# GpSimd, not VectorE, multiplies the edge weights of the first layer's gather quads

## The reference, cut to what matters

```python
deg_out = jax.ops.segment_sum(edge_weight, src, num_segments=N_NODES)
deg_in = jax.ops.segment_sum(edge_weight, dst, num_segments=N_NODES)
norm = edge_weight * jax.lax.rsqrt(deg_out[src] * deg_in[dst] + EPS)

def _gcn_layer(x, W, b, src, dst, norm, n_nodes):
    xt = x @ W
    msg = xt[src] * norm[:, None]
    agg = jax.ops.segment_sum(msg, dst, num_segments=n_nodes)
    return jax.nn.relu(agg + b)
h6 = _gcn_layer(h5_all, W6, b6, src, dst, norm, N_NODES)
h7 = _gcn_layer(h6, W7, b7, src, dst, norm, N_NODES)
```

## Time and profile before

| | |
|---|---|
| runs of the kernel before | 3711.46, 3719.69, 4076.07 us; median 3719.69 us |
| profiled execution, own time | 3675.28 us |
| its span in the profile | 3673.5 us, mean granted clock 0.908 |
| busy PE / DVE / ACT / POOL | 82% / 49% / 31% / 59% of the span |
| gathers of layer 1 | 984, from 491.4 us on |

### The profile page before, as it was taken

The page is one execution under the profiler, slowest core; times in us unless marked ns, Lnnn a source line. Parts: engine busy times, 40 slices in busy tenths (PEclk is TensorE's granted clock), DMA queues, the critical chain, the costliest instruction groups (busy, mean ns, idle before and its releaser), DMA issues.

```text
span 3673.5 us, 51374 instructions
## 1 busy us (share of the span) xinstructions
PE 3014.1 (82%) x16152; PEld 1995.3 (54%) x16152; DVE 1801.7 (49%) x4528; ACT 1146.4 (31%) x4063; POOL 2169.9 (59%) x2090
## 2 busy tenths in 40 slices
PE   4778836888888888888875888888888878888998
PEld 3445524555555555555553555556555546555666
DVE  9989835666666666666541332223212324232334
ACT  5788734444444444344320110002000101012211
POOL 4766656766767677676764666666666666630000
PEclk8899968999999999999987989889888989889999
DMA  4331134454545545445465534654554554533221
GB/s 119 99 102 59 52 78 135 152 164 137 179 141 165 153 140 178 136 152 163 129 208 176 150 105 156 202 187 149 193 191 153 187 159 152 189 112 101 81 77 48
DMA packets 219168, 515.12 MB, mean 140 GB/s; under 512 B 62470, under 2 KB 129461, under 8 KB 207799
## 3 DMA queue, kind: packets, MB, share of 16 engines
q0 software_dynamic: 88704, 243.35, 23.2%
q1 hardware_dynamic: 123683, 261.95, 20.9%
q10 hardware_dynamic: 6500, 6.40, 0.6%
HBM read 384.49 MB, written 127.07 MB: 139 GB/s over the span
## 4 chain that ended last, share of the span: by engine, by line
PE 39%; another core or an unknown queue 5%; issue 5%; DVE 2%; DMA 2%; SPq 1%; ACT 1%; DVEq 0%; ACTq 0%; POOL 0%; POOLq 0%
PE ps L709 17%; PE ps L883 5%; PE ps L670 5%; PE ps L896 5%; PE ps L683 3%; PE ps L816 1%; PE ps L828 1%; PE ps L831 1%; DMA xb<-t 1%; SPq L2054 0%; DMA x2d<-accb 0%; PE ps L648 0%; PE ps L719 0%; PE ps L840 0%
## 5 line engine op out<-in xcount | busy, mean ns | idle before, releaser
L1975 POOL DMA_INDIRECT ringb<-t,src x1848 | 1860.5, 1007 | 939.2 <-issue 499.7
L709 PE MATMUL ps<-xb,ab 125*128 125x256 f32 (+1 forms) x4700 | 1251.2, 405 | 101.1 <-issue 97.7
L709 PEld LDWEIGHTS ps<-xb,ab 125*128 125x128 f32 x4700 | 924.4, 201 | 384.6 <-issue 228.1
L683 PE MATMUL ps<-mlb 128*125 128x300 f32 x1260 | 474.4, 468 | 158.7 <-issue 93.8
L1752 ACT ACTIVATE ab<-ps 125x250 f32 x724 | 294.5, 407 | 753.0 <-PE ps L683 350.4
L670 PE MATMUL ps<-ringb,Sb 128*32 128x257 f32 (+1 forms) x3696 | 374.6, 415 | 89.1 <-issue 60.1
L683 PEld LDWEIGHTS ps<-mlb 128*125 128x125 f32 x1260 | 224.2, 201 | 320.3 <-issue 261.1
L1948 POOL TENSOR_TENSOR ab<-ab,wn 128x100 f32<-128x100 f32 x201 | 274.1, 1369 | 167.6 <-DVE ab L1096 167.6
L610 PE MATMUL ps<-ab 128*50 128x125 f32 x3228 | 222.2, 285 | 132.8 <-ACT ab L1672 47.0
L1282 DVE TENSOR_TENSOR mlb<-iof,rel 128x900 f32<-128x900 f32 (+1 forms) x231 | 232.3, 1005 | 170.2 <-remote 95.0
L1672 ACT ACTIVATE ab<-ab,wn 128x50 f32<-128x50 f32 x1212 | 286.7, 327 | 20.8 <-DVE ab L1096 20.7
(11 more groups left out here) (246 smaller groups left out, 2697.6 us busy)
## 6 DMA issues: line engine op xcount, KB each, us to landing
ad<-ab SPq DMA_DIRECT2D x42, 1600.0 KB
ab<-ad SPq DMA_DIRECT2D x42, 1600.0 KB
ringb<-t,src POOLq DMA_INDIRECT x1848
kvd<-mlb SPq DMA_DIRECT2D x50, 256.0 KB, 2.1
kvb<-kvd SPq DMA_DIRECT2D x50, 256.0 KB
x2t<-mlb SPq DMA_DIRECT2D x13, 500.0 KB
xb<-x2t SPq DMA_DIRECT2D x13, 500.0 KB, 8.2
xb<-in_x SPq DMA_DIRECT2D x10, 625.0 KB
```

Source lines behind the costliest of these rows:

```text
L683: e.matmul(PS[bank_of(t)][0:R, 0:HR], low[:, slot_of(t), :], high[:, slot_of(t), :], start=True, stop=True).then_inc(s_bld, 1)
L709: ins = e.matmul(PS[dense_bank(L, d)][:, 0:wd], lhs, X[0:R, k, 0:wd], start=k == 0, stop=k == NT - 1)
L1975: e.indirect_dma_start(msg[:, slot * QT + k, 0:width], None, table, bass.IndirectOffsetOnAxis(src[:, t:t + 1], 0)).then_inc(s_g[slot], 16)
```

## The change

The 128x4 product moves from DVE to POOL. POOL issues the gathers of quad j and then, between them and the gathers of quad j+1, forms the weights of quad j-1 (`weights_of(j - 1)`): it waits for that quad's gathers to land (`s_g`), from quad 4 on for `s_S`, so that the slot of `wn4` is free, and counts the new semaphore `s_w4`. `wn4` has four slots instead of two. DVE's `weigh_S` waits for `s_w4` and for `equal` and has one instruction less. The path that runs only when the input's order breaks an assumption (`slow_sums`) counts `s_S` too, so that POOL isn't held there; it isn't taken here.

```diff
-        wn4 = sb("wn4", [P, 2, QT])
+        wn4 = sb("wn4", [P, 4, QT])
...
                 if L == 0:
-                    e.wait_ge(s_g[slot], 64 * (j // RQ + 1))
-                    e.tensor_tensor(wn4[:, j % 2, :], wn[:, column(L, j):column(L, j) + QT], msg[:, slot * QT:slot * QT + QT, D + 1],
-                                    ALU.mult).then_inc(s_eq, 1)
-                    e.wait_ge(s_eq, 2 * j + 2)
-                    by = wn4[:, j % 2, :]
+                    e.wait_ge(s_w4, j + 1)
+                    e.wait_ge(s_eq, j + 1)
+                    by = wn4[:, j % 4, :]
                 else:
-                    e.wait_ge(s_eq, 2 * NQ + j + 1)
+                    e.wait_ge(s_eq, NQ + j + 1)
...
+                            if L == 0:
+                                e.sem_inc(s_S, 1)
...
+            def weights_of(j):
+                slot = j % RQ
+                e.wait_ge(s_g[slot], 64 * (j // RQ + 1))
+                if j >= 4:
+                    e.wait_ge(s_S, j - 3)
+                e.tensor_tensor(wn4[:, j % 4, :], wn[:, column(0, j):column(0, j) + QT], msg[:, slot * QT:slot * QT + QT, D + 1],
+                                ALU.mult).then_inc(s_w4, 1)
...
+                    if L == 0 and j >= 1:
+                        weights_of(j - 1)
+                if L == 0:
+                    weights_of(NQ - 1)
```

More of the change, by code:

```diff
@@ L459, in gnn_block @@
         s_g = [sem(f"s_g{i}") for i in range(RQ)]
-        s_eq, s_S, s_mm, s_cp, s_tr, s_add, s_pass = (
-            sem(k) for k in ("s_eq", "s_S", "s_mm", "s_cp", "s_tr", "s_add", "s_pass"))
+        s_eq, s_w4, s_S, s_mm, s_cp, s_tr, s_add, s_pass = (
+            sem(k) for k in ("s_eq", "s_w4", "s_S", "s_mm", "s_cp", "s_tr", "s_add", "s_pass"))
         s_xs, s_M, s_lo, s_L, s_az, s_bld, s_ev, s_c0, s_r0, s_mul, s_lc, s_tc = (
```

## The result

The changed kernel took 3723.10 us (median of 20 runs, 3715.57 to 3736.71), the kernel before 3712.02 us (20 runs beside it, 3706.01 to 4076.07). The ratio is 1.0029, with an interval of 1.0021 to 1.0038: +11 us, clear of zero and far under 2%. The one slow run of 4076.07 us stands outside the ratio, which compares fast runs alone. The profiled execution took 3726.38 us, with a span of 3724.6 us. The 3675.28 us of the profile before were not typical: its 20 timed runs begin at 3706.01. So the 51 us between the two profiled executions are mostly not the change, and where a small difference matters I read the kernel before from two later executions of 3712.44 and 3710.51 us (the first experiment of the first and of the third group).

A forecast was written before the change was run, and what follows sets the result against it. The prediction took PE to set the pace, with POOL second busiest. Start +6, thin slack +5 and DVE -1 gave +10 us: the median 3719.69 becomes 3730, with an 8 in 10 range of 3680 to 3805.

The forecast's parts named there:

- with x of 0 to 0.4, nothing: Layer 1 after the start: if POOL's added time per quad, x, is 0 to 0.4 us, the change costs nothing.
- x = 0.19 + 0.15 + 0.22: POOL's added time per quad in layer 1: product, half a gap and blocking by DVE, 0.56 us.
- The half gap of 0.15: POOL's queue between gathers: one more instruction adds half of a 0.30 us gap, 0.15 us a quad.
- The blocking: POOL's product waits for the end of DVE runs with two SBUF inputs, some 0.22 us a quad.
- Slack: POOL's spare time in layer 1: 127.5 us from 600 to 1900 us, or 0.59 us a quad.
- POOL becomes the bound: Rival, layer 1: x about 1.0, POOL's quad 6.40 us against a 5.99 step, +103 us, 3823; chance 0.15.
- the port: Rival: DVE's runs block POOL's product 0.55 us instead of 0.22, +77 us, 3797; chance 0.09.
- Thin slack, +5 us: The 236 quads after the start: little slack left, so 0.02 us a step, +5 us.
- landings: Rival: crowded DMA queues make the product wait 2 us in every fourth quad, 3837 us; chance 0.04.
- The start, +6 us: Start of layer 1: first weighing 3.4 us later, plus 2.4 over about 6 POOL-bound quads; PE doesn't give it back.
- DVE's relief, -1 us: DVE in layer 1: one instruction less saves 0.06 us a step; taken as -1 us, bounds 0 and -15.
- all 15 us come back: Rival: DVE's 0.06 us return in all steps, POOL stays hidden, -15 + 6 = -9 us, 3711; chance 0.12.

The follow-up runs named there:

- the first experiment of the first and of the third group: The kernel before, unchanged, run again: first group 3709.31 us, ratio 0.9995, beside 3711.19; third group one run, profiled execution 3710.51 us, beside 3716.12.
- end_on_dve: Changed kernel with the products of the last 20 quads of layer 1 (226 to 245) kept on DVE: 3718.69 us, 1.0024 of the kernel before.
- two_behind: Changed kernel with POOL forming the weights of quad j-2, not j-1, behind the gathers of quad j: 3719.17 us, 1.0005 of the kernel before.
- only_end: Changed kernel with POOL forming only the products of quads 226 to 245, DVE all others: 3713.70 us, 1.0011 of the kernel before.
- no_product: Kernel before without the product of line 1239 on any engine, so the source node's factor is left out: 3709.22 us, 0.9995 of the kernel before.
- start_on_dve: Changed kernel with the products of the first 12 quads kept on DVE: 3726.61 us, 1.0041 of the kernel before.
- extra1: Changed kernel with one more such product per quad, to a spare tile, on the faster chip: 3470.55 us, 1.0294 of the kernel before (3372.45).
- extra4: Changed kernel with four more such products per quad, to a spare tile, on the faster chip: 3576.92 us, 1.0611 of the kernel before (3372.45).

## Why the prediction was right, and where its terms were off

The forecast was +10 us and 3730, a kernel that stays within 2%. It measured +11 and 3723.10; the difference of 7 us in the time is that of its base, since the median of three runs was 3719.69 and that of twenty 3712.02. The forecast held, and the last gather of layer 1 starts 9 us later in the mean of the profiles, as told (1992 to 1995 us against 1983 and 1986). Its sum (6 + 5 - 1) did not: the 6 us of the start are nearly absent, the 5 us of the middle are some 9, and some 4 us of the end were in no term. By the prediction's own rule ("with x of 0 to 0.4, nothing") the x that was measured would have made the middle's term 0. That the total came out within 1 us is luck; what held for a reason is that the product stays mostly under POOL's slack.

**What a quad costs POOL, x = 0.19 + 0.15 + 0.22.** The first term was right: minimum 0.202 us, median 0.215. The half gap of 0.15 was wrong in sign: the product sits inside the old gap and leaves 0.17 of 0.30, that is -0.13. The blocking was twice too large: the mean less the median is 0.322 - 0.215 = 0.11 us. So x was 0.19 us instead of 0.56. The step that failed in the blocking is the run of 1.63 us for L1282 + L1284 in the kernel before. A product held by the first of them ends with it and not with the pair, as at 1010.74. Of the 50 products over 0.3 us, 49 ended with the DVE instruction that was running when they began, 38 of these with L1280. Counted as two runs, 156 x (1.091² + 0.542²) / 2 = 116, with 35 for the others 151 / 1300 = 0.12 us, which is what was measured. The Trainium skill says (SBUF — State Buffer, "SBUF: two separate sides", the point on the shared pair) that whichever starts first gets the pair for its whole instruction and the other blocks. Layer 1 agrees with it. It doesn't say which engine gets the pair where one DVE instruction follows the other at once: in layer 1 the product got it, in the 8.83 us of the earlier trace rows it stayed out over several DVE instructions, and it was from these that I took the longer run.

**Slack.** Part of it was used up and most of the rest is seen: with the first later execution, 185.3 - 115 x 0.305 = 150 us of slack, less 211 x 0.19 = 40, leaves 110; after the change 112.9 - 90 x 0.29 = 87 and 20 of landing holds are there. I had forecast waits for others of under 60; they are 112.9, by the same error in x. The step was forecast at 5.97 to 6.03 us and is 6.14, most of it the base again. The rival "POOL becomes the bound" was therefore far off on the chips where the kernel takes 3711 to 3716 us, and so was "the port".

**Thin slack, +5 us.** There is a cost in the middle, 9 us over 226 quads by `end_on_dve`, but not for that reason, since x left much slack. In gathers from 600 to 1900 us it shows as 855 and 851 before against 847, 849 and 848 after: a step of 6.10 against 6.13 us, x 246 = 9 us. (The 5.99 us from which I started was that of the untypical execution.) What goes with it is the rival "landings": I priced it at 2 us in every fourth quad and took it as refuted by three waits in the earlier trace rows. It is 1.7 us in every eighteenth quad (20.1 us, 12 of 211). `two_behind` removes nearly all holds, in the middle and at the end, and with them most of the cost. That the holds cause it is the likeliest reading, not a shown one: `two_behind` also moves the product against everything else, and in 600 to 1900 us DVE waited only 2.1 us for products in the changed kernel, so the path from a held gather to PE is not seen. A wait alone without the product, which would settle it, was not tried.

**TensorE's clock** was in no term, and the measured cost goes with it. The granted clock, as the mean of the timed runs, was 0.9059, 0.9053 and 0.9063 for the kernel before in the three groups on usual chips, and 0.9015, 0.9028 and 0.9020 for the changed kernel. It was 0.9051 in `two_behind`, 0.9054 in `only_end`, 0.9047 in `no_product`, 0.9029 in `end_on_dve` and 0.9042 in `start_on_dve` (five runs). But for the last, the less a variant costs, the nearer it is to the clock of the kernel before. Two traces on the same chip, 600 to 1900 us, before and after (the 0.93 and 0.92 are the clock):

```profile
600.00:1900.00 1300.00, 1105.75 (x5473) 739.60 (x5474) 804.97 (x2192) 527.52 (x1960) 886.54 (x851) 0.93 0.49 150
600.00:1900.00 1300.00, 1093.63 (x5448) 734.48 (x5447) 783.82 (x1963) 523.68 (x1946) 954.75 (x1059) 0.92 0.48 150
```

The clock has two levels, 1.2 and 2.4 GHz. In that stretch it stood at the lower one for 181 and 191 us in the two later executions of the kernel before, for 222, 215 and 208 us in the three of the changed one, and for 188 us in `two_behind`. The multiplications of L709 start 0.43 us apart at the lower level and 0.22 us apart at the higher one (medians), so some 29 us more at the lower level could take up to half of that, 14 us, by an estimate that has PE at work all the time. Within the timed runs of one kernel 0.001 less clock goes with at most 1.5 us more time, which for 0.0035 makes some 5 us. So part of the +11 us may reach the time through the clock. Whether small waits of PE lower it, or it is lowered and makes the waits, no run here separates.

**The start, +6 us.** The mechanism came as told: the first weighing at 502.81 instead of 498.36, +4.4 us for a forecast of 3.4. What failed is the sentence that PE doesn't give the delay back. `start_on_dve` starts at 498.87 as before and ends no earlier. From the first gather to quad 20's matmuls I read 147.8 and 147.3 us before, and 146.2, 151.2 and 148.4 after: the delay is mostly gone by then.

**The end of the layer** was not in the sum. I had treated the 236 quads after the start alike, but in the last ones POOL is behind, holds are frequent, and some 4 us (0.4 to 8) come of the products there; by which path is open.

**DVE's relief, -1 us.** `no_product` gives -2 us with zero inside its interval. The rival that all 15 us come back is refuted. The 0.06 us a step were a misreading, since the two rows compared are of different layers: the weighing starts 0.39 us behind equal after the change too (1004.33 and 1003.94), in the median of all quads 0.389 instead of 0.393, and 0.388 in `no_product`. So the product had added next to nothing between them, and the 0.33 of layer 2 in the earlier trace rows has another reason than its absence.

The chance of 0.19 for over 2% slower was too large for these chips but not for the other one. There `extra1` cost 98.1 us; by 0.144 us for each further product the change itself would cost 98.1 - 0.144 x 246 = 63 us, 1.9%. That is an estimate from `extra1` and `extra4`; the changed kernel alone didn't run there.

## To carry to other kernels

Price a small instruction between two others of an engine by the spacing of starts that it leaves, not by its own length plus a gap: here 0.215 us went in with 0.08 us more from gather to gather, blocking aside. What seems to cost is rather the wait that it brings to the head of an in-order queue: taking data that is one quad older took back 7 to 8 of the 11 us with no more memory. Look where a chain begins before you read shares from it, and compare the granted clock of two kernels as you compare their times. And split a layer into start, middle and end before you share a small cost out over its steps, and measure each by moving only its own steps.

## What the chip showed that I had not expected

The same kernel takes 3711 to 3716 us on three chips and 3372 on a fourth, 339 us less than in the first group of experiments. Layer 1 can't be compared well, since POOL is its bound in all three kernels that were profiled on the fourth chip. In PE's groups from 600 to 1900 us the means are the same; first the kernel before on a usual chip, then `extra1` on the other:

```profile
L709 PE MATMUL ps<-xb,ab 125*128 125x257 f32 x1950 | 501.7, 390 | 6.5 <-issue 6.4
L683 PE MATMUL ps<-mlb 128*125 128x300 f32 x1164 | 435.3, 462 | 128.6 <-issue 64.7 <-ACT side L1756 50.2 <-ACT mlb L1766 7.3
```

```profile
L711 PE MATMUL ps<-xb,ab 125*128 125x257 f32 x2031 | 519.8, 390 | 5.2 <-ACT ab L1754 3.9 <-issue 1.2
L685 PE MATMUL ps<-mlb 128*125 128x300 f32 x1170 | 432.7, 459 | 35.3 <-ACT side L1758 18.1 <-ACT ab L1752 15.6 <-ACT mlb L1768 1.1
```

The means are 390 and 390 ns, 462 and 459. What differs here is the idle time: 64.7 us before line 683 in which PE waited for nothing that the profile shows, and none on the other chip.

The larger part of the gap lies in layer 2, where the kernels run the same instructions. From its first gather to its last it takes 1282 us in the changed kernel of the first group and 1102 us in `extra1`. There the clock and PE's means differ; the row of 2300 to 2500 us and the group of L709 in it, changed kernel and then `extra1`:

```profile
2300.00:2500.00 200.00, 168.79 (x794) 110.70 (x793) 41.05 (x131) 9.40 (x24) 130.49 (x137) 0.88 0.56 184
L709 PE MATMUL ps<-xb,ab 125*128 125x256 f32 x399 | 110.6, 425 | 6.5 <-issue 6.3
```

```profile
2300.00:2500.00 200.00, 180.82 (x986) 127.48 (x985) 71.59 (x228) 26.11 (x78) 152.80 (x156) 0.97 0.61 190
L711 PE MATMUL ps<-xb,ab 125*128 125x256 f32 x483 | 119.6, 394 | 0.0
```

The granted clock is 0.88 against 0.97, and over the whole layer PE stood at the lower level for 280 us against 128. Those 152 us more can make up to 76 of the 180 us, by the same estimate as above. So the clock is one part of the difference between the chips (the kernel before has 0.925 in the mean of 9 runs on the fourth, 0.905 to 0.906 on the others), and not all of it. What makes the clock differ, and what fills the idle time, stays open. With it goes the slack of POOL: 185.3 us of waits for PE in layer 1 on the one, 0.5 us on the other with two products a quad, so that the same added POOL time is mostly hidden on one chip and paid on the other.
